# Layer 1's output projection in four pieces behind the next image's first spreads, and work banks freed one by one

## The chip, the cores and the metric

One core of a Trainium2 chip runs the whole program; seven cores stay idle. The metric is device time in microseconds from the first to the last instruction of that core. The time of the kernel before is 15616.14 us, the median of 3 runs (15596.47 to 15628.25).

## The reference

The input is 8 images of 32 x 32 positions (T = 1024) and 192 channels. Two layers follow each other, each with a residual: x = x + L0(gn(x)), then x = x + L1(gn(x)), where gn is a group norm over 32 groups.

```python
xz = x @ W_in                      # 192 -> 2 * 384; xc is one half, z the other
xc = silu(depthwise_conv3x3(xc))   # 384 channels
# layer 0: K = 8 scan directions, each with weights of its own, N = 16 states per channel
x_dbl = W_x[k] @ xs[k]             # 12 rows for the steps, 16 of B, 16 of C
delta = softplus(W_dt[k] @ dts + bias)
h = exp(delta * A) * h + (delta * u) * B[n]     # along T, for every channel and state n
y = sum over n of h * C[n] + D * u
# layer 1: 4 directions with shared weights, decay = exp(cumsum(delta * A)),
# h = decay * cumsum(delta * u * B / (decay + 1e-12)), y summed likewise
y = layernorm(y) * silu(z)
x = x + y @ W_out                  # 384 -> 192
```

## The kernel before, in words

Channels lie on partitions: 384 channels are J = 3 tiles of 128, and a row of a tile is one picture of 1024 positions. In layer 0 the unit of work is one (direction i, channel tile j, state n): 8 x 3 x 16 = 384 units per image, in the order of the list UNITS. A pass is the 16 units of one (i, j). For each unit:

- SP fetches the row B[n], broadcast to 128 partitions, into one of four buffers (L354), and for units that POOL weighs the row C[n] too, into one of three. `rows0` is the order in which SP issues: row g waits for the source of unit g-4.
- POOL multiplies it by delta*u: the source (`source`, L1166, five buffers). `du` (L1156) makes delta*u of the next pass behind the source of n = 6, once ACT's softplus (L894) of that pass is there.
- ACT writes exp(delta*A) to one of two pairs of PSUM banks: the decay (L911). It waits for the scan of unit g-2.
- DVE runs the recurrence (`scan`, L1335; seven state buffers).
- The state is multiplied by C[n] in one of three ways. For 9 of 16 units DVE does it (`weigh`, L1343) against a row that PE has spread over the partitions in the WORK banks (`spread_c`, L569). For n = 2, 6, 10 (and 12 where j = 0, and now and then 8) POOL does it (`weigh`, L1175), three units behind its sources. For the others PE turns the state into the WORK banks (`turn_state`, L588, eight 128 x 128 transposes) and ACT scales it on the way out (`scale_state`, L929, eight activations).
- PE adds it up in the two YACC banks (`sum_states`: L616 for weighed states, L610 for turned ones). At the end of a pass ACT copies the sum out (`collect`, L936) and the next pass begins (`begin_sums`, L601).

The WORK pair (banks 6 and 7) is shared by spreads, turned states and the side jobs that `piece` places on units no spread is needed for: the step projection of a later pass (`dt`, L541, taken by ACT in L888), x projections, remainders, the turn back of y. `free[h]` remembers what has to be over before bank h is written. `scans0` on each engine is the order, written out by hand: in it PE's step g waits for DVE's weigh of unit g-1 first, then does the piece or spread of g, then the sums that are due, SUM_LAG = 4 units behind (step 4 of a pass has none, step 5 has two). ACT's step g is decay g, then at n = 6 the collect, then what PE's step g-2 left in the WORK banks, then at n = 1 the softplus of the next pass.

Layer 1 (`scans1`, `tail1`) has 48 units of four directions. In `tail1` the next image's front (input projection, convolution, x projection, `head0`) runs inside this image's end. PE's last work there is layer 1's output projection (L777), 12 products of 128 x 512 columns in two halves c = 0 (YACC banks) and c = 1 (WORK banks). It stands behind `head0`'s remainders and ahead of the next image's first spread. ACT copies the halves out in its steps 1 and 2 of the next image (`take_out1`, L1073), DVE adds them to the picture behind the scan of unit 3 (`residual`, L1475), and SP stores the picture ahead of row 13 (`store_out`, L416).

```python
if g == 3 and b > 0:                  # DVE, scans0
    residual(b - 1, 1, 0)
    residual(b - 1, 1, 1)
if g == 12 and b > 0:                 # SP, rows0
    store_out(b - 1)
```

Of the kernel before, what the change touches and what calls it, by code (L numbers as in the profile page):

```python
# [9 lines left out]
P = 128  # L10
# [5 lines left out]
XR = 6 * N  # L16
# [13 lines left out]
POOL_LAG, SUM_LAG = 3, 4  # L30
# [121 lines left out]

def mm(step):

    return "mm0" if step in AHEAD else "mm"


def ev(step):

    return "ev0" if step in AHEAD else "ev"  # L160
# [20 lines left out]
def program(nc, counts, images, x, out, w_in, conv_w, conv_b, w_x0, w_dt0, dt_b0, a_log0, d0,  # L181
# [3 lines left out]
    with ctx:  # L185
# [77 lines left out]
        o2 = room[0:CH, 18:20, :]  # L263
# [3 lines left out]
        def whole(lo):  # L267
# [10 lines left out]
                 "xz", "shift", "silu", "mm", "ev", "mm0", "ev0", "stat0", "stat1", "gs0", "gs1", "xn", "pad", "conv", "u",  # L278
# [26 lines left out]
        def _(sp):  # L305
# [51 lines left out]
            def rows0(b):  # L357
                store_bc(b, 0, 0)
                for g, (i, j, n) in enumerate(UNITS):
# [6 lines left out]
                    if by_pool(i, j, n):  # L366
                        c = POOLED.index((i, j, n))
                        if c == CROWS - 1 and b > 0:

                            sp.wait_ge(S["mm"], at("mm", ("out", 1, 1), b - 1))  # L370
# [63 lines left out]
        def _(pe):  # L434
# [110 lines left out]

            def remainders(b, i, h):
# [37 lines left out]
            def turn_state(b, g):  # L584
                wait_free(0, 1)
                pe.wait_ge(S["scan"], at("scan", UNITS[g], b))
                for k in range(CHUNKS):
                    ins = nc.tensor.matmul(whole(WORK[0])[:, k * P:(k + 1) * P],  # L588
                                           state0[:, g % STATES, k * P:(k + 1) * P], identity[:, :],
                                           start=True, stop=True, is_transpose=True)  # L590
                ins.then_inc(S["turned"], note("turned", UNITS[g]))
                free[0] = free[1] = ("scaled", UNITS[g], b)
# [11 lines left out]
            def sum_states(b, g):  # L604
                i, j, n = UNITS[g]
                if by_turn(i, j, n):
                    pe.wait_ge(S["scaled"], at("scaled", (i, j, n), b))
# [37 lines left out]
            def scans0(b):  # L645
                for g in range(len(UNITS) + SUM_LAG):
# [3 lines left out]
                    if n == SUM_LAG + 1:  # L650
                        begin_sums(b, i, j)
                    p = piece(g)
                    if p:
                        if p[0] == "xd":
                            x_proj(b, p[1], p[2])
                        elif p[0] == "dt":
                            dt_proj(b, 0, p[1], p[2])
# [13 lines left out]
                    if n == SUM_LAG + 1:  # L671
                        sum_states(b, g - SUM_LAG - 1)
                    if g >= SUM_LAG and n != SUM_LAG:
                        sum_states(b, g - SUM_LAG)
# [64 lines left out]

            def tail1(b):  # L740
# [29 lines left out]
                pe.wait_ge(S["load_wout1"], at("load_wout1", 0, b))  # L770
                for c, banks in ((0, (YACC, YACC + 1)), (1, WORK)):
                    if c == 1:
                        wait_free(0, 1)
                    for j in range(J):
                        pe.wait_ge(S["gat"], at("gat", (1, j), b))
                        for h in range(2):
                            ins = nc.tensor.matmul(bank[0:CH, banks[h], :], wout[1][:, j, c * CH:(c + 1) * CH],  # L777
                                                   y[:, j, halves(h)], start=(j == 0), stop=(j == J - 1))
                    ins.then_inc(S["mm"], note("mm", ("out", 1, c)))
                free[0] = free[1] = ("ev", ("out", 1, 1), b)  # L780
# [15 lines left out]
        def _(act):  # L796
# [93 lines left out]

            def softplus(b, i, j):
# [28 lines left out]
            def scale_state(b, g):  # L920
# [5 lines left out]
                act.wait_ge(S["turned"], at("turned", (i, j, n), b))  # L926
                for k in range(CHUNKS):
                    cut = slice(k * P, (k + 1) * P)
# [671 lines left out]
```

## Time and profile before

| | |
|---|---|
| median of 3 runs | 15616.14 us (15596.47 to 15628.25) |
| profiled execution, its own time | 15598.88 us |
| its span, first to last instruction | 15597.0 us |
| mean granted TensorE clock | 0.893 of full speed |
| DVE busy | 13975.7 us (90%) |
| POOL busy | 13678.6 us (88%) |
| PE busy | 12065.7 us (77%) |
| ACT busy | 10298.3 us (66%) |
| DMA | 2440.08 MB, mean 156 GB/s |

Busy shares are means over the whole span. An image takes about 1945 us, of which layer 0's scans take about 1215 us, and the rows further down are read within that stage. "Idle before" is the time that an engine waited ahead of an instruction, with what ended the wait.

### The profile page before, as it was taken

To read this page: it belongs to the slowest core of one execution; us is meant where nothing else is said; L and a number is where in the kernel's file an instruction comes from. 1 tells how busy PE (TensorE), PEld (TensorE's weight loads), DVE (VectorE), ACT (ScalarE), POOL (GpSimd) and SP (SyncE) were. 2 spreads that over 40 slices of the span, in tenths; PEclk is the share of its full clock that TensorE was granted. 3 is DMA by queue.
4 is the path that set the end of the run, shared out by engine and by line. 5 is a ranking of instruction groups with operands and counts; after the bars stand their busy time and mean duration, and the time that the engine had idled before them with its cause. 6 is when DMAs were issued, how large, how long until landed. Compare 5 with 4: busy or idle time off the path is not lost.

```text
span 15597.0 us, 137387 instructions
## 1 busy us (share of the span) xinstructions
PE 12065.7 (77%) x45056; PEld 6526.8 (42%) x45056; DVE 13975.7 (90%) x8019; ACT 10298.3 (66%) x13827; POOL 13678.6 (88%) x5828
## 2 busy tenths in 40 slices
PE   6777877778777787777877878777787777877778
PEld 4443344433444334443344433444334443344433
DVE  8998988989899898998989989899898998989988
ACT  5666766667666676666766667666676666766667
POOL 7997979979899798997889978899789997899978
PEclk8898988989889898898988889889898898988989
DMA  5662255622565225662256622566226662265522
GB/s 184 210 208 97 86 184 208 209 94 86 184 213 209 93 84 189 211 212 89 81 196 210 214 84 78 203 210 210 83 76 210 208 208 81 75 208 208 208 80 76
DMA packets 687758, 2440.08 MB, mean 156 GB/s; under 512 B 78268, under 2 KB 100040, under 8 KB 687048
## 3 DMA queue, kind: packets, MB, share of 16 engines
q1 hardware_dynamic: 687048, 2431.29, 45.0%
q8 instruction: 363, 5.95, 0.2%
q14 instruction: 347, 2.84, 0.1%
HBM read 2415.26 MB, written 15.73 MB: 156 GB/s over the span
## 4 chain that ended last, share of the span: by engine, by line
POOL 38%; DVE 17%; PE 16%; issue 15%; DMA 7%; ACT 6%; DVEq 0%; POOLq 0%; SPq 0%; ACTq 0%
POOL room L1166 21%; DMA room<-bc_rows 7%; POOL room L1209 6%; DVE room L1335 6%; DVE room L1400 5%; PE bank L705 4%; POOL room L1201 3%; POOL room L1212 3%; POOL room L1175 3%; DVE room L1343 2%; PE bank L449 2%; POOL room L1156 2%; PE bank L616 2%; PE bank L610 2%; DVE u L1292 1%
## 5 line engine op out<-in xcount | busy, mean ns | idle before, releaser
L1166 POOL TENSOR_TENSOR room<-room 128x1024 f32<-128x1024 f32 x3072 | 7158.7, 2366 | 0.6
L1335 DVE TENSOR_TENSOR_SCAN room<-bank,room 128x1024 f32<-128x1024 f32 x3072 | 6882.9, 2274 | 212.6 <-ACT bank L911 98.0
L911 ACT ACTIVATE bank<-room,a 128x1024 f32<-128x1024 f32 x3072 | 3409.6, 1126 | 835.8 <-DVE room L1335 816.8
L705 PE MATMUL bank<-room,identity 128*128 128x512 f32 x6144 | 3011.2, 641 | 855.6 <-DVE room L1420 732.8
L1400 DVE TENSOR_TENSOR_SCAN room<-bank,room 128x1024 f32<-128x1024 f32 x1536 | 3430.8, 2273 | 54.0 <-POOL room L1209 33.4
L616 PE MATMUL bank<-identity,room 128*128 128x128 f32 x19456 | 2754.0, 291 | 4.1 <-DVE room L1343 4.1
L1343 DVE TENSOR_TENSOR room<-room,bank 128x1024 f32<-128x1024 f32 x1728 | 2074.6, 1201 | 758.0 <-PE bank L569 753.8
L616 PEld LDWEIGHTS bank<-identity,room 128*128 128x128 f32 x19456 | 2482.3, 152 | 511.1 <-issue 214.4
L705 PEld LDWEIGHTS bank<-room,identity 128*128 128x128 f32 x6144 | 1203.3, 204 | 2663.7 <-issue 1269.6
L1209 POOL TENSOR_TENSOR room<-room 128x1024 f32<-128x1024 f32 x768 | 2238.9, 2938 | 59.9 <-ACT room L1031 30.4
L1175 POOL TENSOR_TENSOR room<-room 128x1024 f32<-128x1024 f32 x704 | 1663.9, 2364 | 342.9 <-DVE room L1335 341.6
L569 PE MATMUL bank<-parts,pick_row 96*128 96x512 bf16 x3456 | 1153.6, 418 | 1047.1 <-ACT room L929 689.9
L929 ACT ACTIVATE room<-bank,c_turned 128x128 f32<-128x128 f32 x5120 | 1389.5, 382 | 720.0 <-PE bank L588 718.3
L610 PE MATMUL bank<-room,identity 128*128 128x512 f32 x2560 | 1512.1, 721 | 18.1 <-DVE room L1343 18.1
L1031 ACT ACTIVATE room<-room,a 128x1024 f32<-128x1024 f32 x1248 | 1365.8, 1138 | 4.5
L1212 POOL TENSOR_TENSOR room<-room 128x1024 f32<-128x1024 f32 x480 | 1152.1, 2410 | 0.0
L588 PE MATMUL bank<-identity,room 128*128 128x128 f32 x5120 | 728.2, 288 | 534.6 <-DVE room L1343 531.6
L569 PEld LDWEIGHTS bank<-parts,pick_row 96*128 96x128 bf16 x3456 | 273.0, 103 | 1849.4 <-ACT room L929 843.7
L1156 POOL TENSOR_TENSOR room<-room,u 128x512 f32<-128x512 f32 x384 | 543.6, 1441 | 571.2 <-ACT room L894 571.2
L1201 POOL TENSOR_TENSOR room<-u,room 128x1024 f32<-128x1024 f32 x384 | 962.7, 2507 | 7.7 <-DMA room<-bc_rows 4.1
L588 PEld LDWEIGHTS bank<-identity,room 128*128 128x128 f32 x5120 | 588.4, 148 | 673.8 <-DVE room L1343 671.3
L610 PEld LDWEIGHTS bank<-room,identity 128*128 128x128 f32 x2560 | 557.0, 232 | 620.4 <-issue 567.7
(131 smaller groups left out, 11438.9 us busy)
## 6 DMA issues: line engine op xcount, KB each, us to landing
room<-bc_rows SPq DMA_DIRECT2D x4544, 512.0 KB, 4.5
wx<-in_w_x SPq DMA_DIRECT2D x65, 162.0 KB
bc_rows<-xdbl SPq DMA_DIRECT2D x72, 128.0 KB, 4.5
pictures<-in_x SPq DMA_DIRECT2D x8, 768.0 KB, 8.8
out_x<-pictures SPq DMA_DIRECT2D x8, 768.0 KB, 7.6
weights<-in_w_in SPq DMA_DIRECT2D x16, 288.0 KB, 6.5
room<-in_w_in SPq DMA_DIRECT2D x16, 288.0 KB, 5.3
room<-in_w_out SPq DMA_DIRECT2D x16, 288.0 KB, 5.9
```

The lines of the kernel that those rows point to most:

```text
L610: ins = nc.tensor.matmul(bank[:, YACC + h, :], identity[:, :], state_turned[:, slot, halves(h)], start=False, stop=False)
L616: ins = nc.tensor.matmul(whole(YACC)[:, k * P:(k + 1) * P], state0[:, g % STATES, k * P:(k + 1) * P], identity[:, :], start=(first_of_layo ...
L705: ins = nc.tensor.matmul(dst, identity[:, :], rhs, start=(q == 0), stop=(q == Q - 1))
L911: nc.scalar.activation(whole(DECAY0[g % 2]), delta0[:, j, :], ACT.Exp, scale=a0[:, col:col + 1]).then_inc(S["decay"], note("decay", (i, j, ...
L1166: nc.gpsimd.tensor_tensor(source0[:, g % SOURCES, :], du0[:, (i * J + j) % 2, :], b_ring0[:, g % BROWS, :], ALU.mult).then_inc(S["source"] ...
L1175: nc.gpsimd.tensor_tensor(state, state, c_ring0[:, c, :], ALU.mult).then_inc(S["weigh_pool"], note("weigh_pool", (i, j, n)))
L1201: nc.gpsimd.tensor_tensor(src, u[:, j, :], b_ring1[:, m % BROWS1, :], ALU.mult).then_inc(S["source1"], note("source1", (j, n)))
L1209: nc.gpsimd.tensor_tensor(state, state, src.rearrange("p (r c) -> p c r", r=SIDE), ALU.mult).then_inc(S["gated"], note("gated", (j, n, q)))
L1212: nc.gpsimd.tensor_tensor(state, state, src, ALU.mult).then_inc(S["gated"], note("gated", (j, n, q)))
L1335: nc.vector.tensor_tensor_scan(run(state0[:, g % STATES, :]), run(whole(DECAY0[g % 2])), run(source0[:, g % SOURCES, :]), 0.0, ALU.mult, A ...
L1343: nc.vector.tensor_tensor(state, state, whole(WORK[0]), ALU.mult).then_inc(S["weigh"], note("weigh", UNITS[g]))
L1400: nc.vector.tensor_tensor_scan(state, dec, state, 0.0, ALU.mult, ALU.add).then_inc(S["scan1"], note("scan1", (j, n, q)))
```

## The change

- **Order.** The sums of a pass are drawn together: units 13 and 14 in step 1 of the next pass, 15 in step 2, and the next pass's sums may begin in step 4. ACT's collect moves from n = 6, straight behind the decay, to n = 4, behind the take of the piece; the softplus moves from n = 1 to n = 2.
- **Banks.** `spread_c`, `turn_state` and the step projection wait for each WORK bank by itself and hand over half by half; ACT scales four chunks as soon as PE has turned them, and takes the step projection in two halves of 512 columns instead of one of 1024.
- **Output projection.** Layer 1's projection is issued in the first four steps of the next image behind their spreads, 4, 2, 2 and 4 of its 12 products, both halves into the YACC banks one after the other. ACT takes them in its steps 2 and 5, DVE adds them behind the scans of units 5 and 9. It has semaphores (mm1, ev1) and a buffer for the result (two rows of y_turned's room) of its own. For the last image it stays in the tail. SP's rows0 is unchanged, with the store still ahead of row 13.

```diff
-POOL_LAG, SUM_LAG = 3, 4
+POOL_LAG = 3
+SUMS0 = {0: (4,), 1: (4, 3), 2: (3,), 3: (), 4: (), 5: (5, 4)}
+LAST_SUM, FIRST_TERM = 2, 4
+OUT1 = {0: (0, (0, 1)), 1: (0, (2,)), 2: (1, (0,)), 3: (1, (1, 2))}
...
+            def dt_by_halves(b, i, j):
+                pe.wait_ge(S[ev(last_xd(0, i))], at(ev(last_xd(0, i)), last_xd(0, i), b))
+                for h in range(2):
+                    step = ("dt", 0, i, j) if h else ("dt_half", i, j)
+                    wait_free(h)
+                    nc.tensor.matmul(bank[:, WORK[h], :], wdt[XR:XR + R, i % 2, j * P:(j + 1) * P],
+                                     xdbl[XR:XR + R, halves(h)], start=True, stop=True).then_inc(
+                        S["mm"], note("mm", step))
+                    free[h] = ("ev", step, b)
...
             def spread_c(b, i, j, n):
-                wait_free(0, 1)
                 if (j, n) == (0, 0):
                     pe.wait_ge(S["parts"], at("parts", (0, i, 1), b))
                 for h in range(2):
+                    wait_free(h)
...
             def turn_state(b, g):
-                wait_free(0, 1)
                 pe.wait_ge(S["scan"], at("scan", UNITS[g], b))
-                for k in range(CHUNKS):
...
+                for h in range(2):
+                    wait_free(h)
+                    for k in range(CHUNKS // 2):
...
+                    ins.then_inc(S["turned"], note("turned", (UNITS[g], h)))
+                    free[h] = ("scaled", (UNITS[g], h), b)
...
             def begin_sums(b, i, j):
...
-                    pe.wait_ge(S["ev"], at("ev", ("out", 1, 0), b - 1))
+                    pe.wait_ge(S["ev1"], at("ev1", ("out", 1, 1), b - 1))
...
+                    if b > 0 and g in OUT1:
+                        out1(b - 1, *OUT1[g])
+                    if n == FIRST_TERM:
+                        begin_sums(b, i, j)
+                    for lag in SUMS0.get(n, (4,)):
+                        if 0 <= g - lag < len(UNITS):
+                            sum_states(b, g - lag)
...
+            def out1(b, c, tiles):
+
+                if c == 1 and 0 in tiles:
+                    pe.wait_ge(S["ev1"], at("ev1", ("out", 1, 0), b))
+                pe.wait_ge(S["load_wout1"], at("load_wout1", 0, b))
+                for j in tiles:
+                    pe.wait_ge(S["gat"], at("gat", (1, j), b))
+                    for h in range(2):
+                        ins = nc.tensor.matmul(bank[0:CH, YACC + h, :], wout[1][:, j, c * CH:(c + 1) * CH],
+                                               y[:, j, halves(h)], start=(j == 0), stop=(j == J - 1))
+                if J - 1 in tiles:
+                    ins.then_inc(S["mm1"], note("mm1", ("out", 1, c)))
...
                 if more:
                     head0(b + 1)
-                pe.wait_ge(S["load_wout1"], at("load_wout1", 0, b))
-                for c, banks in ((0, (YACC, YACC + 1)), (1, WORK)):
...
+                else:
+                    for c in range(2):
+                        out1(b, c, range(J))
...
-                        if n == SUM_LAG + 2 and i * J + j > 0:
-                            collect(b, i * J + j - 1)
...
-                    if g in (1, 2) and b > 0:
-                        take_out1(b - 1, g - 1)
+                    if g in (2, 5) and b > 0:
+                        take_out1(b - 1, int(g == 5))
...
-                        take_dt(b, p[1], p[2])
-
+                        take_dt_by_halves(b, p[1], p[2])
+
+                    if g < len(UNITS) and n == FIRST_TERM and i * J + j > 0:
+                        collect(b, i * J + j - 1)
...
-                    if g < len(UNITS) and n == 1 and 2 <= ahead < PASSES:
+                    if g < len(UNITS) and n == 2 and 2 <= ahead < PASSES:
                         softplus(b, ahead // J, ahead % J)
...
-                if g == 4 and b > 0:
-                    dve.wait_ge(S["res"], at("res", (1, 1), b - 1))
...
-                    if g == 3 and b > 0:
-                        residual(b - 1, 1, 0)
-                        residual(b - 1, 1, 1)
+                    if g in (5, 9) and b > 0:
+                        residual(b - 1, 1, int(g == 9))
```

## Rows read from the trace of the kernel before

**Rows 1.** Stretches, layer 0's scans: span; busy PE, PEld, DVE, ACT, POOL; sum of all eight.
```profile
2004.90:3226.30 1221.40, 929.98 (x4400) 581.30 (x4400) 1099.65 (x605) 769.80 (x1258) 1161.25 (x520) 0.87 0.59 206
...
sum 9729.70, PE 7396.80 PEld 4617.54 DVE 8788.63 ACT 6155.41 POOL 9288.05; mean PE 924.60 PEld 577.19 DVE 1098.58 ACT 769.43 POOL 1161.01
```

**Rows 2.** Waits of POOL, whole span: total us, times, longest.
```profile
POOL room L1156 <- ACT room L894: 571.2, 8, 74.8
POOL room L1175 <- DVE room L1335: 341.6, 175, 12.8
```

**Rows 3.** Waits of DVE, whole span.
```profile
DVE room L1343 <- PE bank L569: 753.8, 379, 16.0
...
DVE room L1335 <- ACT bank L911: 98.0, 171, 0.6
```

**Rows 4.** Timeline, all engines, a turned unit: start, us, engine, line, [idle before].
```profile
2159.06 4.46 DVE L1335 TENSOR_TENSOR_SCAN room<-bank,room 128x1024 f32<-128x1024 f32 x2
...
2159.24 1.07 PE L588 MATMUL bank<-identity,room 128*128 128x128 f32 x8 [0.57 <-DVE room L1343]
...
2160.43 2.17 ACT L929 ACTIVATE room<-bank,c_turned 128x128 f32<-128x128 f32 x8 [1.25 <-PE bank L588]
...
2162.65 0.61 PE L569 MATMUL bank<-parts,pick_row 96*128 96x512 bf16 x2 [0.63 <-ACT room L929]
```

**Rows 5.** Timeline, all engines, the first units of a pass.
```profile
2188.51 1.95 PE L541 MATMUL bank<-xdbl,weights 12*128 12x512 f32 x4 [2.04 <-DVE room L1343]
...
2190.39 2.84 PE L610 MATMUL bank<-room,identity 128*128 128x512 f32 x4
...
2190.50 1.02 ACT L888 ACTIVATE room<-bank 128x1024 f32<-128x1024 f32 x1 [2.05 <-PE bank L541]
...
2193.03 1.06 PE L569 MATMUL bank<-parts,pick_row 96*128 96x512 bf16 x2
```

**Rows 6.** Timeline of DVE, the same pass, its fourth unit's weigh.
```profile
2194.20 1.22 DVE L1343 TENSOR_TENSOR room<-room,bank 128x1024 f32<-128x1024 f32 x1 [1.40 <-PE bank L569]
```

**Rows 7.** Timeline of DVE, the start of the second image.
```profile
2009.89 4.58 DVE L1335 TENSOR_TENSOR_SCAN room<-bank,room 128x1024 f32<-128x1024 f32 x2 [7.68 <-POOL room L1166]
2029.01 1.22 DVE L1343 TENSOR_TENSOR room<-room,bank 128x1024 f32<-128x1024 f32 x1 [14.54 <-PE bank L569]
...
2035.66 4.85 DVE L1475 TENSOR_TENSOR pictures<-pictures,room 96x1024 f32<-96x1024 f32 x2
```

**Rows 8.** Timeline of POOL, the start of the second image.
```profile
2007.45 13.86 POOL L1166 TENSOR_TENSOR room<-room 128x1024 f32<-128x1024 f32 x6
2032.58 2.36 POOL L1175 TENSOR_TENSOR room<-room 128x1024 f32<-128x1024 f32 x1 [11.27 <-DVE room L1335]
...
2037.18 4.44 POOL L1156 TENSOR_TENSOR room<-room,u 128x512 f32<-128x512 f32 x2
...
2061.46 2.36 POOL L1175 TENSOR_TENSOR room<-room 128x1024 f32<-128x1024 f32 x1 [1.28 <-DVE room L1335]
```

**Rows 9.** Timeline of PE, the start of the second image.
```profile
2016.04 11.15 PE L777 MATMUL bank<-y,room 128*96 128x512 f32 x24
```

**Rows 10.** Timeline of ACT, the start of the second image.
```profile
2016.14 0.59 ACT L882 ACTIVATE parts<-bank 32x512 bf16<-32x512 f32 x1 [1.68 <-PE bank L560]
...
2029.56 1.15 ACT L894 ACTIVATE room<-room,dtb 128x1024 f32<-128x1024 f32 x1
2030.72 1.28 ACT L911 ACT_TABLE_LOAD   x1
```

**Rows 11.** Timeline of SP, issue of the store at the start of the second image.
```profile
2047.12 0.43 SPq L416 DMA_DIRECT2D out_x<-pictures  x1
```

**Rows 12.** Line L354, the row issued at 2048.58: time to landing.
```profile
DMA to landing us min/median/max: 7.3/7.3/7.3
```

**Rows 13.** Line L1475, all 32: duration in ns, minimum, median, maximum.
```profile
L1475 DVE TENSOR_TENSOR pictures<-pictures,room x32: 1220/1222/2647, 1325.7 to 15591.0; 96x1024 f32<-96x1024 f32 x32
```

**Rows 14.** Timeline of DVE, the end of the first image's layer 0 scans.
```profile
1279.92 1.22 DVE L1343 TENSOR_TENSOR room<-room,bank 128x1024 f32<-128x1024 f32 x1 [2.83 <-PE bank L569]
```

More of the change, by code:

```diff
@@ L150 @@
     (name, 0, h) for name in ("rest", "last") for h in range(2)}
+LATE = {("out", 1, 0), ("out", 1, 1)}
 def mm(step):
-    return "mm0" if step in AHEAD else "mm"
+    return "mm0" if step in AHEAD else "mm1" if step in LATE else "mm"
 def ev(step):
-    return "ev0" if step in AHEAD else "ev"
+    return "ev0" if step in AHEAD else "ev1" if step in LATE else "ev"
 class Counts:
@@ L584, in turn_state @@
             def turn_state(b, g):
-                wait_free(0, 1)
                 pe.wait_ge(S["scan"], at("scan", UNITS[g], b))
-                for k in range(CHUNKS):
[L588 to L592, printed above, removed]
+                for h in range(2):
+                    wait_free(h)
+                    for k in range(CHUNKS // 2):
+                        cut = slice((h * CHUNKS // 2 + k) * P, (h * CHUNKS // 2 + k + 1) * P)
+                        ins = nc.tensor.matmul(whole(WORK[0])[:, cut], state0[:, g % STATES, cut], identity[:, :],
+                                               start=True, stop=True, is_transpose=True)
+                    ins.then_inc(S["turned"], note("turned", (UNITS[g], h)))
+                    free[h] = ("scaled", (UNITS[g], h), b)
             def begin_sums(b, i, j):
@@ L645, in scans0 @@
             def scans0(b):
-                for g in range(len(UNITS) + SUM_LAG):
+                for g in range(len(UNITS) + LAST_SUM + 1):
                     i, j, n = UNITS[g] if g < len(UNITS) else (K, 0, g - len(UNITS))
@@ L656, in scans0 @@
                         elif p[0] == "dt":
[L657 removed]
+                            dt_by_halves(b, p[1], p[2])
                         elif p[0] == "rest":
@@ L769, in tail1 @@
                     head0(b + 1)
-                pe.wait_ge(S["load_wout1"], at("load_wout1", 0, b))
-                for c, banks in ((0, (YACC, YACC + 1)), (1, WORK)):
[L772 to L780, printed above, removed]
+                else:
+                    for c in range(2):
+                        out1(b, c, range(J))
             pe.wait_ge(loaded, 16 * LOADS)
@@ L889, in take_dt, with take_dt_by_halves @@
                     S[ev(step)], note(ev(step), step))
+            def take_dt_by_halves(b, i, j):
+                for h in range(2):
+                    take(b, ("dt", 0, i, j) if h else ("dt_half", i, j), delta0[:, j, halves(h)], h)
             def softplus(b, i, j):
@@ L925, in scale_state @@
                     act.wait_ge(S["sum"], at("sum", TURNED[t - TURNS], b))
-                act.wait_ge(S["turned"], at("turned", (i, j, n), b))
-                for k in range(CHUNKS):
-                    cut = slice(k * P, (k + 1) * P)
-                    ins = nc.scalar.activation(state_turned[:, t % TURNS, cut], whole(WORK[0])[:, cut],
-                                               ACT.Identity, scale=c_turned[:, i % 2, k, n:n + 1])
-                ins.then_inc(S["scaled"], note("scaled", (i, j, n)))
+                for h in range(2):
+                    act.wait_ge(S["turned"], at("turned", ((i, j, n), h), b))
+                    for k in range(h * CHUNKS // 2, (h + 1) * CHUNKS // 2):
+                        cut = slice(k * P, (k + 1) * P)
+                        ins = nc.scalar.activation(state_turned[:, t % TURNS, cut], whole(WORK[0])[:, cut],
+                                                   ACT.Identity, scale=c_turned[:, i % 2, k, n:n + 1])
+                    ins.then_inc(S["scaled"], note("scaled", ((i, j, n), h)))
             def collect(b, pass_):
@@ L1095, in take_out1 @@
             def take_out1(b, c):
-                take_pair(b, ("out", 1, c), o2[:, c, :], ((YACC, YACC + 1), WORK)[c], rows=CH)
+                take_pair(b, ("out", 1, c), o2[1][:, c, :], (YACC, YACC + 1), rows=CH)
             def tail0(b):
@@ L1103, in tail0 @@
                 for c, banks in ((0, WORK), (1, SPARE)):
-                    take_pair(b, ("out", 0, c), o2[:, c, :], banks, rows=CH)
+                    take_pair(b, ("out", 0, c), o2[0][:, c, :], banks, rows=CH)
             def tail1(b):
```

23 lines of the change are left out of this document (9 added, 14 removed).

## The prediction

> **What bounds the kernel now.** I read three views: the stretches of layer 0's scans, the waits of POOL and DVE, and the timeline where they meet. The stretches show the eight scan stages, 1216 us each (9729.7 / 8), in which POOL is busy 1161 us, DVE 1099 us, PE 925 us and ACT 769 us [rows 1]. So POOL is the floor of the stage, though DVE has the greater share of the whole span, and the most that the stages can give back is what they last over POOL's work: 9729.7 - 9288.05 = 441.7 us. POOL's waits say where it is: 341.6 us before its weighs, for a scan of DVE [rows 2]. The other 100 us, 12.5 a stage, are DVE's end behind POOL's last source.
>
> Why is DVE late? It waits 753.8 us before its weighs for PE's spread, 379 times, 2.0 us each, and 98.0 us for decays [rows 3]. DVE's own work is 62 us a stage less than POOL's. A stall of DVE costs something only where it uses up this slack and the lag that POOL allows (its weigh of unit g-3 stands behind source g). POOL's long wait at a stage's start, 571.2 us for the softplus L894, lies in the tail of the image before, which the change leaves as it is up to that point [rows 2].
>
> There are three kinds of stall:
> - **A turned unit.** Between the weigh before and the weigh behind it DVE has two scans, 4.46 us. In them PE turns (1.07), ACT scales (2.17) and PE spreads (0.61): issued 0.2 us behind the weigh, the spread ends 4.2 us later, just in time [rows 4]. That is at 2.4 GHz; at 1.2 GHz PE's two parts double and the spread is 1.5 us late.
> - **The head of a pass.** PE's projection takes 1.95 us, ACT's copy 1.02, but PE spreads only at 2193.03, since the sum of the turned unit 14 stands in between (2.84 us, begun at 1.2 GHz's pace) [rows 5]. DVE waits 1.40 us [rows 6].
> - **The image's start.** Scans 0 and 1 are over at 2014.47, the first weigh starts at 2029.01: 14.54 us, since PE first does the 12 products of the projection in 11.15 us [rows 7, 9]. POOL loses 11.27 us of it [rows 8].
>
> **The change, part by part.** Times are those of the second image.
>
> *Start, projection behind the spreads.* ACT's last copy of parts ends at 2016.73 [rows 10]; the first spread (about 1.0 us at 1.2 GHz, 0.61 at 2.4) can follow, so weigh 0 starts near 2018.0 and scan 2 is over near 2021.4. POOL's six sources end at 2021.3 [rows 8], so the 11.27 us go. But four things now come late:
> - ACT's softplus of pass 1 stands behind its copy of half c = 0, which needs 6 of 12 products, 5.6 us, and a spread: 2024.2. Copy (1.0), table load (1.28) and softplus (1.15) [rows 10] end near 2027.7, and du, due at 2026, waits 1.7 us for it. Du itself falls from 4.44 us [rows 8] to the 2.5 us of two undisturbed halves, since no residual runs beside it.
> - Decay 3 comes near 2030, scan 3 with it, against 2033.46 now, the end of weigh 1 and scan 2 behind the first weigh [rows 7]. Scans 3 to 6, weigh 3 and a residual bring scan 6 to 2041. POOL, through with source 9 near 2037, waits 4 us for it.
> - DVE's second residual moves from the place of 2038 to behind scan 9. Scans 7 to 9 and weighs 5 and 7 (3 x 2.2 + 2 x 1.1) and a residual put its end near 2051.7.
> - **The store.** SP issues it now at 2047.12 without a wait [rows 11]; later it waits for that residual, and rows 13 and on wait behind SP. I take the issue at 2052.0. The row issued 1.46 us behind the store today landed 7.3 us later [rows 12], so 8.8 us behind the store; with the queue empty before it I take 6 to 8.8. Row 13 lands near 2058 to 2061, source 13 ends near 2062, and POOL's weigh 10 follows where it now starts at 2061.46 [rows 8].
> So the start gives and takes the same: **0 us**, bounds from the rows: 8 us gained an image (the wait of 11.27 without the new ones of DMA) to 8 us lost (the last pieces at 1.2 GHz, twice 5.6 us for six products).
>
> The residual adds two SBUF tiles. It takes 1.22 us alone [rows 13], 4.85 us for two beside POOL's du [rows 7], whose halves then take 2.2 instead of 1.25 us [rows 8]. Beside sources it should cost POOL 1.2 us each, as it costs du now, so nothing is gained or lost. The Trainium skill (SBUF — State Buffer, Who interferes with whom) says that a VectorE instruction with two SBUF inputs and a GpSimd instruction that reads SBUF block each other for a whole instruction; the trace agrees. By that rule each residual may also wait out a source (2.3 us) and the store leaves up to 4.6 us later, which would make the sum some 20 us smaller.
>
> *Order and halves in the passes.* Of the 341.6 us, seven starts take about 79 (7 x 11.27); 262 are left, 33 an image. DVE's stalls in the passes are 753.8 - 7 x 14.5 + 98.0 = 750 us, 94 a stage.
> - A turned unit by halves: ACT begins after four transposes, PE spreads bank 6 while ACT scales bank 7. At 1.2 GHz the spread then ends at 0.2 + 1.0 + 2.2 + 0.5 + latencies of 0.4 = 4.3 us, inside DVE's 4.46. These stalls go.
> - The projection by halves costs ACT 0.2 us more per piece (two of 0.6 for one of 1.02; 184 of them, under other work of ACT, which is busy 769 of 1216 us). The sum of unit 14 leaves the gap; the shorter one of unit 15, eight transposes, takes its place. From the end of weigh 1 the spread of unit 3 ends at 0.2 + 1.95 + 1.04 + 0.6 = 3.8 us, inside 4.46; at 1.2 GHz at 7.4, 3 us late. This stall shrinks to a fifth.
> - The softplus one unit later: the decay it holds up is now due behind scan, weigh, scan, weigh and weigh, 7.7 us, and needs 1.1 + 3.7 + 1.1 = 5.9. The 0.58 us go.
> - The collect now stands before decay 5. It needs the sum of unit 15, 0.2 + 1.95 + 1.04 us behind weigh 1 at best; copy and decay follow in 2.1 + 0.3, together 5.6, where DVE has 2 scans and weigh 3 = 5.5. So scan 5 is met at 2.4 GHz and 3 us late at 1.2; PE is at 1.2 GHz for a quarter of the stage (PEclk 0.87 to 0.88 [rows 1] is 0.5 for 0.25 of the time). That is a new stall of 0.8 us a pass, 19 a stage.
> DVE's stalls in the passes thus fall from 94 to about 45 us. DVE and its stalls are then 1145 us against POOL's 1161, so DVE paces only for short stretches, and of POOL's 33 us I leave 9. **8 x 24 = 192 us gained**; bounds 0 (POOL's waits stay) and 262.
>
> *End of the stage.* The last weigh waits 2.83 us for its spread [rows 14], which stands behind the turned unit 14. By halves this nearly goes: 2.5 of the 12.5 us, **8 x 2.5 = 20 us**; bounds 0 and 5 an image.
>
> *Last image.* Half c = 1 goes to the banks of c = 0, so its products wait for ACT's copy: **1 us lost**, once.
>
> **Sum.** 192 + 20 + 0 - 1 = 211 us. The profiled execution took 15598.88 us (span 15597.0, 2 us around it), 17 us under the median; the change is 1.35% of either. 15616.14 - 211 = **15405 us**.
>
> TensorE's clock: in a stage PE is at 2.4 GHz for three quarters of the time and falls after short waits. The Trainium skill (TensorE: Matmul & The Clock Gate, Part 1) says that idleness drops the clock and activity brings it back. By that rule fewer PE waits would mean more time at 2.4 GHz, and the new stall of 19 us a stage would shrink; the sum would be up to 40 us better. I don't count on it.
>
> **Rivals.**
> - *A: POOL never waits.* PE's halves and a better clock free DVE fully, POOL's 262 us go, the ends shrink by 5 each, the starts gain 3: 15616 - 262 - 40 - 21 = 15293. For it: POOL has more work than DVE in every stage [rows 1]. Against it: the collect's new place and the store.
> - *B: the starts and the clock eat it.* Only half of 262 comes back, since the stalls at a pass's head last (ACT takes the pieces in its order, which halves do not change), and each start loses 5: 15616 - 131 - 10 + 35 = 15510. For it: du waits, scan 6 is late and row 13 is late, all three in a row.
> - *C: slower.* ACT's collect before decay 5. Where PE is at 1.2 GHz at the heads of the passes, scan 5 is 3 to 4 us late in each of 24: 84 us a stage; with the 41 that I leave elsewhere (other stalls and the start) DVE's stage is 1099 + 125 = 1224, 8 more than now: 15616 + 64 = 15680. It decides from 4.9 us of DVE stall a pass, above which DVE paces the stage and today's 1216 is passed. Against it: PE is busy 925 of 1216 us and at 2.4 GHz for most of it.
> - *D: no effect.* The halves only shift the waits (DVE waits as long elsewhere) and the start breaks even: 15616, 15585 to 15647.
>
> **Numbers.** My case 0.58, A 0.13, B 0.18, D 0.06, C 0.05. The forecast's own range is 15350 to 15460. Down to A's 15293 and up past B's 15510 the range is 15290 to 15540, which leaves out C, D and the edges. A measurement tells a change from none at about 0.2%, 31 us. Faster by more than that: 0.58 + 0.13 + 0.18 = 0.89, less 0.01 for B's edge; within: 0.07; slower: 0.05.
>
> **What would show it.** In the waits, DVE's L1343 behind PE's spread falls from 753.8 to under 300 us and POOL's wait for scans from 341.6 to 70 to 150, most of it in the first 15 units of images 2 to 8. A new wait of POOL's source for the DMA of the row appears, once an image, 6 to 10 us: if not, the store's step is wrong. POOL's busy time in a stage stays 1161 us. DVE waits for POOL's sources more than now. A new wait of the scan for decay 5 shows C's place. The forecast is wrong if POOL waits as long as now although DVE's stalls have gone, or if the wait for the row is over 12 us.

## The result and the profile after

The changed kernel takes 15373.55 us (median of 4 runs, 15369.67 to 15377.06) against 15618.88 us in the same comparison: 245 us less, ratio 0.9845, 95% interval 0.9828 to 0.9862. The forecast was 15405 us, 211 us less; the range of 15290 to 15540 holds the result. A second comparison gave 15367.8 us and a ratio of 0.984 (0.9823 to 0.9856).

The stretches of layer 0's scans, as in [rows 1] (span; busy PE, PEld, DVE, ACT, POOL; sum of all eight):

```profile
1972.60:3158.60 1186.00, 910.83 (x4400) 585.10 (x4400) 1098.52 (x605) 775.03 (x1280) 1158.90 (x520) 0.89 0.63 212
...
sum 9500.40, PE 7295.10 PEld 4662.89 DVE 8781.09 ACT 6197.95 POOL 9272.51; mean PE 911.89 PEld 582.86 DVE 1097.64 ACT 774.74 POOL 1159.06
```

The eight stages take 9500.4 us instead of 9729.7: 229.3 us less, and that is the whole difference of the profiled spans (15597.0 to 15367.9). The medians differ by 16 us more, since the profiled execution of the kernel before took 20 us less than its median and that of the changed kernel 4 us less. POOL's work in them is what it was. What the stages last over it fell from 441.7 to 227.9 us.

The waits of POOL and DVE, as in [rows 2, 3]; L1209 is POOL's weigh, L1200 its source, L1190 du, L1375 DVE's weigh, L1367 the scan:

```profile
POOL room L1190 <- ACT room L927: 517.9, 14, 76.3
...
POOL room L1209 <- DVE room L1367: 64.8, 29, 5.7
POOL room L1200 <- DMA room<-bc_rows: 47.3, 5, 9.9
...
POOL room L1200 <- DVE room L1367: 18.3, 2, 9.2
```

```profile
DVE room L1375 <- PE bank L591: 321.6, 289, 4.0
DVE room L1367 <- issue: 185.9, 229, 1.7
...
DVE room L1367 <- ACT bank L944: 115.7, 83, 6.4
DVE room L1367 <- POOL room L1200: 102.9, 32, 16.2
```

POOL's wait for scans fell from 341.6 to 64.8 us and DVE's for spreads from 753.8 to 321.6. The second row of DVE is new (185.9 us, where it was 16.0). In 227 of its 229 waits the scan starts 0.09 us behind the end of its own source, so DVE is waiting for POOL there. With the fourth row, DVE's scans wait 286.1 us for sources, where it was 92.5 us: POOL now sets the pace of much of the stage. Seven waits ahead of a source are new, 65.6 us: source 13 of images 2 to 8, five named by the row's DMA and two by a scan that had long been done.

The start of the second image on POOL and DVE, as in [rows 7, 8]:

```profile
1989.29 2.35 POOL L1209 TENSOR_TENSOR room<-room 128x1024 f32<-128x1024 f32 x1 [0.25 <-DVE room L1367]
...
1996.21 2.47 POOL L1190 TENSOR_TENSOR room<-room,u 128x512 f32<-128x512 f32 x2 [2.26 <-ACT room L927]
...
2011.34 2.38 POOL L1209 TENSOR_TENSOR room<-room 128x1024 f32<-128x1024 f32 x1 [5.72 <-DVE room L1367]
...
2029.85 2.37 POOL L1200 TENSOR_TENSOR room<-room 128x1024 f32<-128x1024 f32 x1 [9.17 <-DVE room L1367]
2032.17 2.36 POOL L1209 TENSOR_TENSOR room<-room 128x1024 f32<-128x1024 f32 x1
```

```profile
1985.72 1.22 DVE L1375 TENSOR_TENSOR room<-room,bank 128x1024 f32<-128x1024 f32 x1 [3.53 <-PE bank L591]
...
1998.59 4.47 DVE L1367 TENSOR_TENSOR_SCAN room<-bank,room 128x1024 f32<-128x1024 f32 x2 [6.37 <-ACT bank L944]
...
2008.91 2.29 DVE L1367 TENSOR_TENSOR_SCAN room<-bank,room 128x1024 f32<-128x1024 f32 x1 [1.42 <-ACT bank L944]
...
2020.87 1.20 DVE L1507 TENSOR_TENSOR pictures<-pictures,room 96x1024 f32<-96x1024 f32 x1
```

SP and ACT in the same place, as in [rows 10, 11]:

```profile
2022.09 0.34 SPq L428 DMA_DIRECT2D out_x<-pictures  x1
2022.47 10.09 SPq L366 DMA_DIRECT2D room<-bc_rows  x5
```

```profile
1992.65 1.02 ACT L1107 ACTIVATE room<-bank 96x1024 f32<-96x1024 f32 x1 [7.19 <-PE bank L772]
1993.69 1.28 ACT L927 ACT_TABLE_LOAD   x1
```

All of the start's late things are there: du waits 2.26 us for the softplus, which stands behind ACT's copy; scan 3 waits 6.37 us for its decay; POOL waits 5.72 us for scan 6; and source 13 waits 9.17 us, since SP could issue row 13 only at 2022.47, behind the store, and it landed 7.2 us later. In sum POOL's weigh 10 stands 59.6 us behind the stage's first instruction (2032.17 - 1972.62), where it stood 56.6 us behind it before (2061.46 - 2004.9). Before, the second image had one of the two shortest starts, and others took up to 58.1 us; over the seven images weigh 10 stands 2.1 us later in the mean.

### The profile page after: what moved, and what is told of

The parts are those of the page before. It is cut to its first block, busy times and chain, and to the rows that moved or that the text cites. A ratio compares the mean times of both kernels' runs of the same rounds, so it can differ in the third digit from the quotient of the medians.

```text
span 15367.9 us, 137305 instructions
## 1 busy us (share of the span) xinstructions
PE 11967.6 (78%) x45056; PEld 6572.3 (43%) x45056; DVE 13967.1 (91%) x8019; ACT 10340.9 (67%) x14003; POOL 13665.7 (89%) x5828
## 4 chain that ended last, share of the span: by engine, by line
POOL 47%; issue 18%; DMA 11%; DVE 10%; PE 10%; ACT 3%; SPq 0%; POOLq 0%; DVEq 0%; ACTq 0%
POOL room L1200 25%; DMA room<-bc_rows 11%; POOL room L1243 7%; POOL room L1209 4%; POOL room L1246 4%; POOL room L1235 4%; DVE room L1431 4%; PE bank L729 3%; POOL room L1190 2%; PE bank L461 2%; DVE room L1367 2%; DVE u L1326 1%; DVE room L1451 1%; DVE room L1440 1%; DVE room L1375 1%
## 5 line engine op out<-in xcount | busy, mean ns | idle before, releaser
L1367 DVE TENSOR_TENSOR_SCAN room<-bank,room 128x1024 f32<-128x1024 f32 x3072 | 6909.9, 2276 | 426.1 <-issue 185.9
L1200 POOL TENSOR_TENSOR room<-room 128x1024 f32<-128x1024 f32 x3072 | 7179.2, 2386 | 66.2 <-DMA room<-bc_rows 47.3
L729 PE MATMUL bank<-room,identity 128*128 128x512 f32 x6144 | 3012.0, 641 | 854.1 <-DVE room L1451 729.0
L639 PE MATMUL bank<-identity,room 128*128 128x128 f32 x19456 | 2851.8, 297 | 4.3 <-DVE room L1375 4.1
L639 PEld LDWEIGHTS bank<-identity,room 128*128 128x128 f32 x19456 | 2554.9, 156 | 524.1 <-issue 310.2
L1375 DVE TENSOR_TENSOR room<-room,bank 128x1024 f32<-128x1024 f32 x1728 | 2072.3, 1199 | 323.8 <-PE bank L591 321.6
L729 PEld LDWEIGHTS bank<-room,identity 128*128 128x128 f32 x6144 | 1203.3, 204 | 2663.1 <-issue 1267.4
L591 PE MATMUL bank<-parts,pick_row 96*128 96x512 bf16 x3456 | 1249.5, 423 | 738.4 <-DVE room L1375 440.0
L1209 POOL TENSOR_TENSOR room<-room 128x1024 f32<-128x1024 f32 x704 | 1680.3, 2387 | 64.9 <-DVE room L1367 64.8
L612 PE MATMUL bank<-identity,room 128*128 128x128 f32 x5120 | 804.1, 308 | 983.4 <-DVE room L1375 982.9
L633 PE MATMUL bank<-room,identity 128*128 128x512 f32 x2560 | 1310.0, 637 | 4.1 <-DVE room L1375 4.1
L612 PEld LDWEIGHTS bank<-identity,room 128*128 128x128 f32 x5120 | 646.5, 159 | 1169.0 <-DVE room L1375 1163.0
L1190 POOL TENSOR_TENSOR room<-room,u 128x512 f32<-128x512 f32 x384 | 534.2, 1425 | 588.7 <-ACT room L927 517.9
L591 PEld LDWEIGHTS bank<-parts,pick_row 96*128 96x128 bf16 x3456 | 326.7, 103 | 1480.4 <-DVE room L1375 588.5
L828 ACT ACTIVATE room<-bank 128x512 f32<-128x512 f32 x544 | 323.7, 598 | 720.9 <-PE bank L563 317.5
```

Source lines behind the costliest of these rows:

```text
L639: ins = nc.tensor.matmul(whole(YACC)[:, k * P:(k + 1) * P], state0[:, g % STATES, k * P:(k + 1) * P], identity[:, :], start=(first_of_layo ...
L729: ins = nc.tensor.matmul(dst, identity[:, :], rhs, start=(q == 0), stop=(q == Q - 1))
L1200: nc.gpsimd.tensor_tensor(source0[:, g % SOURCES, :], du0[:, (i * J + j) % 2, :], b_ring0[:, g % BROWS, :], ALU.mult).then_inc(S["source"] ...
L1209: nc.gpsimd.tensor_tensor(state, state, c_ring0[:, c, :], ALU.mult).then_inc(S["weigh_pool"], note("weigh_pool", (i, j, n)))
L1367: nc.vector.tensor_tensor_scan(run(state0[:, g % STATES, :]), run(whole(DECAY0[g % 2])), run(source0[:, g % SOURCES, :]), 0.0, ALU.mult, A ...
L1375: nc.vector.tensor_tensor(state, state, whole(WORK[0]), ALU.mult).then_inc(S["weigh"], note("weigh", UNITS[g]))
```

## The experiments

Twelve runs, each against the kernel before on the same chip. Ratios have their 95% intervals. They come from three chips, on which the median of the kernel before is 15614.1, 15621.5 and 15645.2 us, so medians of two chips can't be compared to 20 us. Where it matters I go by the stages of the profiles: outside the eight stages every profile spends 5859 to 5871 us.

**Projection back in the tail; order and halves stay.**

```diff
-                    if b > 0 and g in OUT1:
-                        out1(b - 1, *OUT1[g])
...
+                pe.wait_ge(S["load_wout1"], at("load_wout1", 0, b))
+                for c, banks in ((0, (YACC, YACC + 1)), (1, WORK)):
```

> The changed kernel with layer 1's output projection back in the tail, one piece ahead of the first spread; order and halves stay. My theory (the gain comes from the passes, and the start gives as much as it takes): 15355 us, between 15335 and 15380, since POOL's weigh 10 stood 56.6 us behind the stage's first instruction before and stands 59.6 us behind it now, 3 us later in seven images. POOL waits some 12 us for scan 2 in each of seven starts and never for the row 13. Rival (the moved projection carries a good part of the gain, since the 11.27 us wait at the start is gone): 15430 to 15455 us.

Measured: 15351.57 us, ratio 0.9813 (0.9798 to 0.9827). POOL's waits:

```profile
POOL room L1192 <- DVE room L1352: 111.2, 30, 13.0
```

The wait at the start is back (up to 13.0 us), the one for row 13 is gone, and the kernel is faster than the changed one: 16 us in the medians against the second comparison (another chip) and 22 against the first, 42 to 50 us by the ratios, 27 to 29 us in the profiles' spans (15338.7 against 15367.9 and 15365.5). The ratio's interval ends below that of the first comparison of the changed kernel (0.9828) and overlaps that of the second by 0.0004. In the profiles the starts of the seven images are 19 us shorter in sum, 2.7 us each. So the moved projection has no part in the gain, and in the profiles it costs a little. My theory held, the rival fell.

**Whole pairs of banks; order and projection stay.**

```diff
             def turn_state(b, g):
+                wait_free(0, 1)
...
-                for h in range(2):
-                    wait_free(h)
```

> The changed kernel with whole pairs of banks again for spreads, turned states and the step projection; new order and projection stay. My theory (the halves take away the stalls of turned units at the low clock and of the pass's head): DVE's wait for spreads goes back from 322 to 550 us or more, POOL's wait for scans to 200 us or more, 15480 us, between 15430 and 15530. Rival (the order alone does it, the halves are hidden): 15375 to 15395 us.

Measured: 15428.63 us, ratio 0.9865 (0.9851 to 0.988). That is nearer to my theory than to the rival, but 1.4 us below the range that I gave. The sizes of the waits were wrong: DVE's wait for spreads is 459.1 us and POOL's for scans 124.5, both below what I gave.

**Old order; halves and projection stay.**

```diff
-                    for lag in SUMS0.get(n, (4,)):
...
+                    if n == SUM_LAG + 1:
+                        sum_states(b, g - SUM_LAG - 1)
```

> The changed kernel with the sums, the collect and the softplus at their old units; halves and projection stay. My theory (the order is the lesser part): 15430 us, between 15395 and 15470; the wait of scan 2 for its decay comes back (0.58 us in most passes), the wait of weigh 3 too, the new waits of scans 3 and 5 for decays go. Rival (the order costs as much as it gives, as the collect now holds up decay 5): 15365 to 15385 us.

Measured: 15449.71 us, ratio 0.9876 (0.9861 to 0.9891). The value is as expected, but not the ranking. On the same chip taking out the order cost 21 us more than taking out the halves in the medians, and as much in the profiled executions (spans 15445.5 and 15445.2; that of the halves is the slowest of its four). The order is no lesser part. The waits of weigh 3 and scan 2 came back (54.9 and 3.9 us a stage) and that of scan 5 went, as expected; that of scan 3 was to go and stayed at 6.4 us, all of it at the start.

**The store four rows later.** It now stands behind row 16, so ahead of row 17; the expectation says 16.

```diff
-                    if g == 12 and b > 0:
+                    if g == 16 and b > 0:
```

> The changed kernel with SP's store of the picture ahead of row 16 instead of row 13. My theory (row 13 waits 7 to 9 us behind the store in seven images, and POOL keeps what it gets back of it until DVE, with 36 us of slack a stage, sets the pace): POOL's wait of 9.2 us ahead of source 13 goes, its weigh 10 waits 1 to 2 us for scan 10; 15330 us, between 15318 and 15350. Rival (DVE is as late as POOL there, so the wait only changes its name): 15360 to 15375 us.

Measured: 15337.31 us, ratio 0.9802 (0.9786 to 0.9819). POOL at the start of the second image:

```profile
2009.42 2.38 POOL L1203 TENSOR_TENSOR room<-room 128x1024 f32<-128x1024 f32 x1 [5.07 <-DVE room L1361]
2011.76 10.31 POOL L1194 TENSOR_TENSOR room<-room 128x1024 f32<-128x1024 f32 x4
2022.18 2.35 POOL L1203 TENSOR_TENSOR room<-room 128x1024 f32<-128x1024 f32 x1
```

Source 13 runs straight behind source 12, in all seven images. The kernel gains some 30 us in the medians and 25 in the spans (59 to 67 by the ratios, as this chip is the slowest of the three); the other part of the 65.6 us turned up as waits for scans, 102.0 us instead of 64.8. The time is in the range that I gave. But the rival has a share in it, and the traces show how large. The seven starts are 50 us shorter and not 65.6, since weigh 10 waits 3.4 us for scan 10 in images 3, 6, 7 and 8 (in the second image, above, it doesn't): there DVE's second residual takes 3.2 us instead of 1.4. And behind unit 15 POOL's waits rise from 24 to 49 us. The third image's residual and weigh 10:

```profile
3930.86 3.22 DVE L1501 TENSOR_TENSOR pictures<-pictures,room 96x1024 f32<-96x1024 f32 x1
...
3936.43 2.36 POOL L1203 TENSOR_TENSOR room<-room 128x1024 f32<-128x1024 f32 x1 [3.42 <-DVE room L1361]
```

**The changed kernel once more**, for the comparisons of the next three.

> The changed kernel once more, so that the parts are compared on the same chip: 15373 us and up to 0.3% beside it where this chip is a little slower, a ratio of 0.983 to 0.986; its profile as on record, POOL waiting 9 us ahead of source 13 in seven images.

Measured: 15367.8 us, ratio 0.984 (0.9823 to 0.9856), span 15365.5 us.

**Each part alone on the kernel before.** The diffs are the hunks of one part.

> The kernel before with the output projection behind the next image's spreads alone; old order, whole pairs of banks. My theory (the start breaks even, the passes stay as they were): 0 to 20 us faster than before, ratio 0.999, between 0.997 and 1.001; POOL's waits for scans stay above 230 us and the row 13 is waited for in most of seven images. Rival (the projection is worth the 11.27 us a start): 75 us faster, ratio 0.995.

Measured: 15602.52 us (10 runs), ratio 0.999 (0.9981 to 1.0): no effect on the time. The waits changed their names: 11.27 us a start became 67.0 us in seven waits for row 13, while the passes kept theirs.

```profile
POOL room L1186 <- DVE room L1344: 287.1, 176, 6.5
...
POOL room L1177 <- DMA room<-bc_rows: 67.0, 7, 10.2
```

> The kernel before with the new order of sums, collect and softplus alone. My theory (order and halves work on the same wait of POOL for DVE's scans, and either alone gets most of it since POOL is the floor): 150 to 190 us faster than before, ratio 0.989, between 0.987 and 0.991. Rival (they add up, as they take different stalls of DVE): what taking the order out cost, 75 to 80 us, ratio 0.995.

Measured: 15436.36 us, ratio 0.9882 (0.9868 to 0.9897), 178 us less than before. POOL's wait for scans fell to 178.0 us.

> The kernel before with the work banks freed and handed over by halves alone. My theory (as for the order alone: POOL is the floor, so the first part gets the most): 150 to 190 us faster than before, ratio 0.989, between 0.987 and 0.991. Rival (the parts add up): 75 to 80 us faster, ratio 0.995.

Measured: 15444.28 us, ratio 0.9886 (0.9872 to 0.9901), 170 us less. DVE's waits fell by 90 us for spreads and 64 for decays, and POOL's for scans by 140, so nearly all of it reached POOL. With the order alone DVE's fell by 240 and 51 us (to 514.1 and 47.3) and POOL's by 164.

```profile
POOL room L1191 <- DVE room L1351: 201.4, 120, 13.0
...
DVE room L1359 <- PE bank L579: 663.5, 289, 16.2
```

In spans, order and halves alone give 167 and 159 us, together (without the projection) 258, and each costs 77 to 80 when it is taken out of the whole (in the medians 76 to 82 and 55 to 61). They don't add up: in the passes either one alone takes more than half of what POOL waits (the last table of this section). The rival of adding parts fell, twice.

To see which waits each part takes, I grouped the idle time of DVE and POOL in the traces by the unit it stands before: us per stage, mean of images 2 to 7, over all passes. Weigh 3 is the weigh of the unit n = 3 of a pass.

```text
                      before   only order   only halves   changed
scan 2                 12.1        0.0          4.2          0.0
scan 5                  0.0        5.1          0.0          5.5
weigh 0                15.4       15.3         15.6          3.5
weigh 3                53.3        3.9         53.3          2.8
weigh 5                 2.4       18.7          0.0          9.5
weigh 7                 5.0       11.7          2.0         10.6
weighs 9, 13, 15       16.2       16.5         12.2          9.8
all weighs of DVE      94.2       66.8         85.2         40.5
POOL, for scans/rows   43.3       24.8         27.5         18.1
```

The order alone empties the head of the pass (weigh 3: 53.3 to 3.9) and makes a new stall before weigh 5. Ahead of its spread PE turns unit 4 and begins the sums, as it did in the kernel before, but at another pace. Here is one such place in the kernel before, then one with the order alone:

```profile
2195.52 1.06 PE L588 MATMUL bank<-identity,room 128*128 128x128 f32 x8
2196.49 1.98 PE L601 MATMUL bank<-room,identity 128*128 128x512 f32 x4
```

```profile
2756.24 1.94 PE L590 MATMUL bank<-identity,room 128*128 128x128 f32 x8 [1.82 <-DVE room L1344]
2757.97 3.62 PE L603 MATMUL bank<-room,identity 128*128 128x512 f32 x4
```

In the second, PE has waited 1.82 us, and the granted clock of the stretch is 0.50 of full speed (1.2 GHz); DVE's weigh 5 waits 1.92 us there. Over all passes a product that begins the sums takes 592 ns in the median before and 980 with the order alone. The halves alone leave weigh 3 as it is; added to the order, they halve its new stall.

**The two kinds of halves, and the softplus.** First whole pairs for turned states and spreads alone (the edit of "Whole pairs of banks" without the step projection's part):

> The changed kernel with whole pairs of banks for turned states and spreads; only the step projection stays halved. The halves together were worth some 60 us beside order and projection. My theory (they work where a turned unit and the begin of the sums stand ahead of the spread of unit 5): nearly all of that is lost, 15420 us, between 15400 and 15440. Rival (the projection's halves do it, at the head of the pass): 15368 to 15385 us.

Measured: 15414.07 us, ratio 0.9863 (0.9847 to 0.988).

Then the step projection alone as a whole:

```diff
-                            dt_by_halves(b, p[1], p[2])
+                            dt_proj(b, 0, p[1], p[2])
```

> The changed kernel with the step projection taken as a whole again; turned states and spreads stay halved. My theory: the order has already emptied the pass's head, 15375 us, between 15360 and 15390. Rival: 15410 to 15430 us.

Measured: 15375.04 us, ratio 0.9839 (0.9824 to 0.9853). So the halves' value beside the order, some 40 to 46 us in the medians, lies in the turned states and spreads; no run parts these two. The step projection's halves are worth nothing that can be measured.

```diff
-                    if g < len(UNITS) and n == 2 and 2 <= ahead < PASSES:
+                    if g < len(UNITS) and n == 1 and 2 <= ahead < PASSES:
```

> The changed kernel with the softplus back at n = 1; sums and collect stay at their new units. The order together was worth some 80 us beside the rest. My theory: the sum of unit 14 out of the gap is what counts, the softplus is worth its 0.5 us a pass and not all of that: 15383 us, between 15368 and 15400; scan 2 waits 0.5 us for its decay again. Rival (the softplus carries the order's gain): 15420 to 15450 us.

Measured: 15373.93 us, ratio 0.9838 (0.9823 to 0.9853): nothing. Scans wait 130.5 us for decays instead of 115.7, which the time doesn't show. So the order's value lies in the sums and the collect, which no run parts.

**A version that beats both.** With the store behind row 16, ACT copies the projection's first half behind decay 3.

```diff
-                    if g in (2, 5) and b > 0:
+                    if g in (3, 5) and b > 0:
```

> The kernel with the store ahead of row 16, and ACT's copy of the projection's first half one step later, behind decay 3, so that the softplus of pass 1 and decay 3 don't wait for it. My theory (ACT's order is what holds du and scan 3 at the start): du's wait of 2.3 us goes, scan 3 starts some 3 us earlier, POOL's wait for scan 6 falls from 5.7 to about 3 us, 15320 us, between 15305 and 15333. Rival (PE's twelve products set the start, not ACT's order): 15333 to 15345 us.

Measured: 15315.78 us (15305.58 to 15318.23), ratio 0.98 (0.9786 to 0.9815): 52 to 58 us faster than the changed kernel in the medians, 62 to 64 in the spans. POOL and DVE at the start:

```profile
1997.83 2.49 POOL L1184 TENSOR_TENSOR room<-room,u 128x512 f32<-128x512 f32 x2
2000.27 7.97 POOL L1194 TENSOR_TENSOR room<-room 128x1024 f32<-128x1024 f32 x3
2008.81 2.37 POOL L1203 TENSOR_TENSOR room<-room 128x1024 f32<-128x1024 f32 x1 [0.57 <-DVE room L1361]
```

```profile
1998.71 2.29 DVE L1361 TENSOR_TENSOR_SCAN room<-bank,room 128x1024 f32<-128x1024 f32 x1 [0.28 <-ACT bank L938]
...
2004.29 1.74 DVE L1501 TENSOR_TENSOR pictures<-pictures,room 96x1024 f32<-96x1024 f32 x1
...
2018.33 3.20 DVE L1501 TENSOR_TENSOR pictures<-pictures,room 96x1024 f32<-96x1024 f32 x1
```

Du waits for nothing, scan 3 no longer waits for its decay (the row above is scan 4's, 0.28 us), and POOL's wait for scan 6 is 0.57 us, less than the 3 us I expected (0.4 to 0.6 in six images, 3.4 in the fourth). What is left at the start is a wait of 3.4 us in each of the seven images: for scan 10 in six, behind a second residual of 3.2 us, and for scan 6 in the fourth, behind a first residual of 3.0 us. No run has ACT's later copy without the later store.

**Where the time of the stages is lost, kernel by kernel.** From the traces, us in sum. "Start" is the time from POOL's first instruction of a stage to its source 16, for images 2 to 8. "Waits later" are POOL's from there on, "end" is what DVE still does behind POOL's last instruction, both for all eight stages. "Order and halves" is the run with the projection back in the tail.

```text
                               start   waits later    end
before                         467.3         248.0   98.2
only projection                486.0         245.1   97.2
only order                     465.4          86.2   98.9
only halves                    463.4         113.0   82.5
order and halves               462.6          22.0   81.4
changed (all three)            481.7          23.8   81.4
changed, store later           431.5          48.6   76.8
the same, ACT's copy later     395.1          54.0   78.1
```

The projection acts on the starts and makes them 19 us longer, both alone (467.3 to 486.0) and with the other two parts (462.6 to 481.7). The order takes 162 us of the waits later and the halves 135, together 226 of the 248 that there were. The shorter ends are the work of the halves.

## Why the prediction was right, point by point

- **POOL is the floor, and only what the stages last over its work can come back.** Right: its busy time in the stages moved by 0.2%, and 214 of the 441.7 us above it came back (the other 15.5 us of the 229.3 are POOL's own busy time). DVE's scans now wait 286 us for POOL's sources. Order and halves each take more than half of POOL's waits when alone, and together they can't take more than there is.
- **Start, forecast 0, bounds 8 us an image either way.** The steps came nearly as worked out. The second image's stage begins 32.3 us earlier; with that shift weigh 0 was forecast at 1985.7 and came at 1985.72, the store at 2019.7 and came at 2022.09, row 13 was to land 6 to 8.8 us behind the store and did so after 7.6. Over seven images the sum is 14 us worse than break-even, 2.1 us each, and 2.7 us each against the run without the projection.
- **Order and halves in the passes, forecast 192 us: too small.** POOL's waits behind unit 15 fell from 248.0 to 23.8 us, by 224. The forecast had DVE's own stalls there fall from 94 to about 45 us a stage; by the traces they fell from 93.7 to 44.6. Its last step was mis-sized: of POOL's 33 us a stage I left 9, and these 45 us of stalls cost POOL only 3. What there was to gain I had put too high, 262 us instead of 248, since I took the second image's wait of 11.27 us for all seven, which lose up to 12.8 and then 1.3 more.
- **Which stalls go: partly wrong, so that the total of 45 us is in part luck.** I had turned units at the low clock stand beside the pass's head as a cause. The head was over half of it (weigh 3, 53.3 of 94.2 us a stage), and the order took it. The stalls that I had said would go, those behind turned units 8, 12 and 14 (weighs 9, 13 and 15), were 16.2 us and are 9.8. I had looked for the order's new stall at scan 5, behind the collect, 19 us a stage: it is 5.5 there and 9.5 at weigh 5, together 15. The wait of weigh 7 doubled, from 5.0 to 10.6 us, for which I had nothing. The step projection's halves and the softplus, which I counted as gains of DVE, are worth nothing.
- **End of the stage, forecast 2.5 us each.** What the stages last over POOL's work and waits fell from 12.5 to 10.2 us: 2.3 us. It is the halves, as said: the last weigh waits 1.4 us with them and 2 to 3 without.
- **Last image, forecast 1 us.** PE's second half now waits 1.11 us for ACT's copy.
- **The sum.** The passes gave 32 us more than forecast, the starts took 14 and the ends gave 3 less; that is 15 of the 18 us by which the stages beat the forecast, and errors of opposite sign made it look better than its terms. The other 16 us between forecast and result come with the profiled executions and not with the stages, as said above.
- **The signs given.** L1343's successor was to fall under 300 us and is at 321.6; POOL's wait for scans was to fall to 70 to 150 and is at 64.8; the wait for row 13 was to be 6 to 10 us an image and is 9.4 (65.6 / 7). DVE does wait for POOL's sources more than before.
- **Rivals.** A has the passes right (POOL hardly waits there) and the starts wrong. B named three late things at the start that all came, but the passes gave more than half. C's stall is there at under a fifth of its price, 15 us of 84, counting that of weigh 5. D fell with the result. TensorE's clock moved from 0.893 to 0.899, and I had not counted on it. It is hardly the main cause: the order alone gives 178 us at 0.894. How much it gave beside that no run tells.

What stays open: which stall of DVE costs POOL what. With the halves alone nearly all that DVE's waits lost came back to POOL, with the order alone little more than half, and the waits that rise from 24 to 49 us when the store stands later were not traced to one stall.

## What to carry to other kernels

Where two engines are nearly balanced, take the one with more work in the stage as the floor, and ask of each stall of the other whether it uses up the slack; two edits that take different stalls can then give less together than the sum of each alone (here 258 us for 167 and 159). When work is moved behind something on one engine, follow its result through every queue in order: here the gain of 11.27 us at each start was given back by a store that stood ahead of a row it had nothing to do with (9.4 us), and by a copy that stood ahead of a softplus and a decay (2.2 and 5.7). Moving that one issue and one copy was worth some 60 us. A wait in the order of SP's issues holds up all loads behind it (here SP issued nothing from 2008.59 to 2022.09), so put it where they have the most slack. And read all the images: in the second one alone, with the store later, weigh 10 seems never to wait.

## What the runs showed of the hardware that was not expected

The residual add at the start took 1.20 us in the changed kernel (1.42 in one of 14), where POOL stood still for lack of a scan or a row, and 1.74 and 3.20 us in the second image of the last version, where POOL's sources ran beside it. Beside the first, three sources took 7.97 us instead of 6.99; beside the second, four took 9.31, about what they take undisturbed (9.28), so that DVE alone lost time. That is the blocking between a VectorE instruction with two SBUF inputs and GpSimd's reads which the Trainium skill (SBUF — State Buffer, Who interferes with whom) describes; that the changed kernel escapes it only because POOL is waiting was not foreseen. For the first add the price is near the 1.2 us that the prediction took. For the second it is not: DVE loses 2 us, and POOL's weigh 10 then waits 3.4 us for the scan behind it, where it waits 0.1 us when the add takes 1.8 (fourth image).
